# Two subtractions moved to GpSimd, a ring of eight PSUM banks and a new order of the steady period in an attention and gate kernel

## The reference

```python
xn = _layernorm(x, axis=-1)
q, k, v = proj(Wq), proj(Wk), proj(Wv)            # of xn
scores = einsum('bhsd,bhtd->bhst', q, k)          # causal
attn = softmax(where(mask, -inf, scores) / sqrt(D))
s = einsum('bse,fe->bsf', attn @ v, Wo)
h = silu(einsum(xn, wg)) * einsum(xn, wu)         # hidden 768, int weights / 127
g = _silu(einsum('bsh,dh->bsd', h, wd))
out = x + s * g
```

## Time and profile before

| | us |
|---|---|
| median of 3 runs (945.82 to 946.13) | 945.88 |
| the profiled execution's own time | 947.55 |
| its span, first to last instruction | 945.8 |
| TensorE busy | 914.8 (97%) |
| VectorE busy | 707.2 (75%) |
| ScalarE busy | 585.8 (62%) |
| GpSimd busy | 495.1 (52%) |

### The profile page before, as it was taken

How to read it: one execution, slowest core, us unless ns; L and a number is a source line. 1 busy time by engine, 2 the same in 40 slices (tenths; PEclk the granted TensorE clock), 3 DMA queues, 4 the chain that set the end, 5 groups by cost and what they waited for, 6 DMA issues and landing times.

```text
span 945.8 us, 22760 instructions
## 1 busy us (share of the span) xinstructions
PE 914.8 (97%) x9065; PEld 685.6 (72%) x9065; DVE 707.2 (75%) x950; ACT 585.8 (62%) x796; POOL 495.1 (52%) x681
## 2 busy tenths in 40 slices
PE   3999999999999999999999999999999999999995
PEld 2777767776868777686877868777786867768654
DVE  5985868778696887868788786877778697776823
ACT  5356664757576675756657575665757557575771
POOL 4253553736456464645636455473745547364553
PEclk9999999999999999999999999999999999999999
DMA  6704235353353534535343453534345253543323
GB/s 221 213 25 170 84 116 169 100 198 132 134 164 127 170 106 179 154 125 171 129 151 126 170 152 117 176 132 158 130 148 162 104 185 120 175 131 135 118 93 98
DMA packets 84507, 133.97 MB, mean 142 GB/s; under 512 B 13680, under 2 KB 34928, under 8 KB 84336
## 3 DMA queue, kind: packets, MB, share of 16 engines
q1 hardware_dynamic: 84400, 132.47, 41.8%
HBM read 53.22 MB, written 25.75 MB: 83 GB/s over the span
## 4 chain that ended last, share of the span: by engine, by line
PE 91%; DVE 2%; DMA 2%; POOL 2%; issue 1%; ACT 1%; SPq 0%; POOLq 0%; ACTq 0%; DVEq 0%
PE bank L194 48%; PE values L525 15%; PE bank L434 12%; PE bank L492 11%; PE bank L447 4%; DMA o_reciprocals<-scratch_r 1%; ACT probs L500 1%; DVE row_max L457 1%; PE bank L463 1%; POOL o_compact L566 1%; PE bank L668 0%; DMA scratch_r<-sum_reciprocals 0%; DVE x_in L259 0%; DVE xt_lo L279 0%; DMA sums<-scratch_o 0%
## 5 line engine op out<-in xcount | busy, mean ns | idle before, releaser
L457 DVE TENSOR_REDUCE row_max<-bank 128x2 f32<-128x768 f32 (+3 forms) x352 | 384.9, 1124 | 63.5 <-PE bank L447 60.3
L500 ACT ACTIVATE probs<-bank 128x1024 f32<-128x1024 f32 x320 | 320.4, 1026 | 122.2 <-PE bank L492 120.8
L507 POOL TENSOR_SCALAR_AFFINE_SELECT probs<-probs 128x256 f32<-128x256 f32 (+1 forms) x448 | 194.0, 450 | 275.1 <-ACT probs L500 274.1
L525 PE MATMUL values<-probs,v 128*17 128x512 f32 (+3 forms) x2048 | 166.2, 436 | 0.9 <-POOL probs L507 0.9
L393 POOL TENSOR_TENSOR h_lo<-gated,h_hi 128x512 fp32r<-128x512 f32 x96 | 124.6, 1298 | 74.8 <-ACT h_hi L390 72.7
L434 PE MATMUL bank<-k_stack,q_stack 64*128 64x128 f32 (+3 forms) x1024 | 155.3, 363 | 1.5 <-DVE row_max L457 1.2
L492 PE MATMUL bank<-q_stack,k_stack 64*128 64x512 f32 (+3 forms) x1024 | 142.2, 350 | 1.3 <-DVE row_max L457 0.7
L434 PEld LDWEIGHTS bank<-k_stack,q_stack 64*128 64x128 f32 x1024 | 83.1, 186 | 66.9 <-issue 30.4
L492 PEld LDWEIGHTS bank<-q_stack,k_stack 64*128 64x128 f32 x1024 | 82.9, 186 | 39.1 <-issue 17.3
L366 DVE SCALAR_TENSOR_TENSOR gated<-gated,bank 128x512 f32<-128x512 f32 x96 | 65.8, 685 | 55.4 <-ACT gated L363 55.4
L194 PE MATMUL bank<-xt_hi,wg_hi 128*128 128x256 f32 x384 | 99.3, 293 | 1.6 <-DVE gated L379 1.6
(11 more groups left out here) (123 smaller groups left out, 1624.4 us busy)
## 6 DMA issues: line engine op xcount, KB each, us to landing
k_stack<-qk_hi SPq DMA_DIRECT2D x64, 256.0 KB, 2.5
q_stack<-qk_hi SPq DMA_DIRECT2D x64, 256.0 KB, 2.5
scratch_o<-o SPq DMA_DIRECT2D x64, 256.0 KB, 2.2
x_again<-x SPq DMA_DIRECT2D x16, 512.0 KB, 4.7
k_stack<-qk_lo SPq DMA_DIRECT2D x32, 256.0 KB, 2.5
q_stack<-qk_lo SPq DMA_DIRECT2D x32, 256.0 KB, 2.6
o_compact<-scratch_o SPq DMA_DIRECT2D x32, 256.0 KB
o_reciprocals<-scratch_r SPq DMA_DIRECT2D x32, 256.0 KB
```

The source lines that it names most:

```text
L457: signal(e.tensor_reduce(rows, scores, axis=AX.X, op=ALU.max), "d_sm")
L500: signal(e.activation(PR[:, (SCORES * beta + k) % SLOTS, :, :], both(banks), ACT.Exp, scale=SCALE_S), "d_ex")
L507: last = e.affine_select(out=diag, in_=diag, compare_op=ALU.is_ge, fill=0.0, base=0, pattern=[[0, many], [1, P]], channel_multiplier=-1)
L525: last = nc.tensor.matmul(PVB[32 * c:32 * c + VW, j * P:S], V[par][:, j, 4 * g + c, :], PR[:, (SCORES * beta + 5 * g + kind) % SLOTS, pari ...
```

## The change

1. The low part of x (`lx`) and of the attention output (`os`) are subtracted by GpSimd instead of VectorE, in all three tables.
2. The bank of its own for values is gone. PSUM is one ring of 8 banks, and each `pv` entry names its bank. In HEAD and TAIL that is always bank 7, so only the name changes there; `pv` waits by `prev` now.
3. PERIOD has a new order and new banks. TAIL differs in two places: `os 1 1` now stands behind `on 1 1`, and the last `op` names bank 7 as well.

```diff
-RELEASED = dict(..., st="d_ex")
-RING = 7
+RELEASED = dict(..., st="d_ex", pv="d_ov")
+RING = 8
...
 PERIOD = table("""
-    ld 2 0, on 0 0, zr 0 0, ob 0 0, pv 0 11, sm 1 16 45, lt 2 0, st 1 1 01, la 2 0, st 1 2 23, mk 1 16 45, lm 2 0, gg 1 3 6,
+    on 0 0, ld 2 0, ob 0 0, lt 2 0, pv 0 11 7, lm 2 0, la 2 0, st 1 1 01, st 1 2 23, sm 1 16 45, mk 1 16 45, gu 1 2 6,
...
 TAIL = table("""
...
-    hs 1 4, ob 1 1, gu 1 5 0, hs 1 5, zr 0 0, os 1 1, xr 1 0, zr 1 0, on 1 1, dn 1 1 6, op 1 0 1, op 1 1 4""")
+    hs 1 4, ob 1 1, gu 1 5 0, hs 1 5, zr 0 0, xr 1 0, zr 1 0, on 1 1, os 1 1, dn 1 1 6, op 1 0 1, op 1 1 47""")
...
-        PVB = ctx.enter_context(nc.psum_tensor("values", [P, 512], FP32))
...
 def u_lx: 
-            elif en == "dve":
+            elif en == "pool":
                 after(e, "d_xh", beta, 1)
                 e.tensor_tensor(r(XT[1][:]), XTR[:], XT[0][:], ALU.subtract).then_inc(sems["d_xl"], 2)
...
 def u_pv:
                 if part == 0:
-                    after(e, "d_ov", beta, g - 1)
+                    prev(e)
...
-                            last = nc.tensor.matmul(PVB[32 * c:32 * c + VW, j * P:S], V[par][:, j, 4 * g + c, :],
+                            last = nc.tensor.matmul(PS[32 * c:32 * c + VW, banks[0], j * P:S], V[par][:, j, 4 * g + c, :],
...
-                signal(e.activation(O[:], PVB[:], ACT.Copy), "d_ov")
+                signal(e.activation(O[:], PS[:, banks[0], :], ACT.Copy), "d_ov")
...
 def u_os:
-            elif en == "dve":
+            elif en == "pool":
                 after(e, "d_oh", beta, k)
                 signal(e.tensor_tensor(r(OT[1][:, k, :]), OC[:], OT[0][:, k, :], ALU.subtract), "d_ol")
...
-                return PVB[:, 0:E] if halves and j == 1 else PS[:, banks[0], j * E:(j + 1) * E]
+                return PS[:, banks[1], 0:E] if halves and j == 1 else PS[:, banks[0], j * E:(j + 1) * E]
...
-                    users.update((n, (kind, b + ahead, k)) for n in banks)
+                    users.update((n, (kind, b + ahead, k // 3 if kind == "pv" else k)) for n in banks)
```

More of the change, by code:

```diff
@@ new lines @@
+    st 1 7 23, sm 1 21 45, mk 1 21 45, st 1 8 01, v 2 0 6, mt 1 1 2, gg 2 0 3, pv 1 3 7, sm 2 0 01, sm 2 1 45, or 0 1,
+    mk 2 0 01, hs 1 5, ob 0 1, mk 2 1 45, st 1 9 23, qk 2 2 6, pv 1 4 7, st 1 10 23, st 1 11 45, on 0 1, sm 2 2 01, mk 2 2 01,
+    pv 1 5 7, gu 2 0 6, st 1 12 01, st 1 13 34, os 0 1, od 1 0, pv 1 6 7, sm 2 3 01, mk 2 3 01, sm 2 4 56, mk 2 4 56, st 1 14 34,
+    qk 2 3 2, ls 2 2, dn 1 1 3, sm 2 5 56, st 1 15 01, pv 1 7 7, or 1 0, mk 2 5 56, sm 2 6 34, ls 2 3, st 1 16 01, mk 2 6 34,
@@ L80 @@
+    op 0 0 2, sm 2 7 01, st 1 17 45, mk 2 7 01, op 0 1 6, sm 2 8 45, hs 2 0, sm 2 9 01, mk 2 8 45, st 1 18 23, pv 1 8 7,
     mk 2 9 01, sm 2 10 45, sm 2 11 23, xr 1 0, mk 2 10 45, mk 2 11 23, st 1 19 01, gg 2 1 6, mt 2 0 4, sm 2 12 01,
[L81 to L82 removed]
+    mk 2 12 01, gu 2 1 5, v 2 1 3, sm 2 13 01, mk 2 13 01, sm 2 14 45, hs 2 1, mk 2 14 45, gg 2 2 6, pv 1 9 7, sm 2 15 01,
@@ L84 @@
+    mk 2 15 01, st 2 0 34, pv 1 10 7""")
 PERIOD = table("""
[L85 to L88 removed]
@@ new lines @@
+    gg 1 3 7, st 1 3 01, lc 2 0, sm 1 17 23, gu 1 3 4, mk 1 17 23, sm 1 18 56, st 1 4 01, mk 1 18 56, hs 1 2, gg 1 4 7,
+    gu 1 4 4, gg 1 5 2, zr 0 0, gu 1 5 3, lb 2 0, sm 1 19 01, st 1 5 56, od 0 1, mk 1 19 01, pv 1 0 7, pv 1 1 7, sm 1 20 23,
+    st 1 6 01, sm 1 21 45, lx 2 0, mk 1 20 23, os 0 0, mk 1 21 45, dn 1 0 6, mt 1 1 0, pv 1 2 7, pv 1 3 1, hs 1 3, st 1 7 23,
+    st 1 8 45, ls 2 0, st 1 9 67, qk 2 0 0, ls 2 1, v 2 0 2, hs 1 4, qk 2 1 3, hs 1 5, or 0 1, gg 2 0 4, gg 2 1 5, gg 2 2 6,
@@ new lines @@
+    ob 0 1, qk 2 2 7, st 1 10 23, st 1 11 45, pv 1 4 1, pv 1 5 1, st 1 12 67, sm 2 0 23, od 1 0, mk 2 0 23, sm 2 1 45,
+    ls 2 2, on 0 1, mk 2 1 45, qk 2 3 0, gu 2 0 1, sm 2 2 67, os 0 1, sm 2 3 23, sm 2 4 45, mk 2 2 67, mk 2 3 23, mk 2 4 45,
+    dn 1 1 0, st 1 13 67, sm 2 5 12, sm 2 6 34, ls 2 3, mk 2 5 12, mk 2 6 34, op 0 0 5, op 0 1 6, sm 2 7 01, st 1 14 23,
+    mk 2 7 01, sm 2 8 45, mk 2 8 45, pv 1 6 7, st 1 15 23, xr 1 0, sm 2 9 01, mk 2 9 01, hs 2 0, pv 1 7 7, pv 1 8 7,
+    sm 2 10 45, mk 2 10 45, or 1 0, st 1 16 23, st 1 17 01, gu 2 1 6, mt 2 0 7, st 1 18 45, sm 2 11 23, mk 2 11 23,
@@ new lines @@
+    sm 2 12 01, hs 2 1, mk 2 12 01, v 2 1 6, sm 2 13 45, st 1 19 23, mk 2 13 45, pv 1 9 7, sm 2 14 01, mk 2 14 01, st 2 0 23,
+    sm 2 15 45, mk 2 15 45, pv 1 10 7""")
+TAIL = table("""
+    ob 0 0, st 1 1 23, sm 1 16 45, on 0 0, mk 1 16 45, st 1 2 01, pv 0 11 7, sm 1 17 56, od 0 1, mk 1 17 56, st 1 3 34,
+    sm 1 18 12, mk 1 18 12, os 0 0, pv 1 0 7, st 1 4 56, st 1 5 01, sm 1 19 34, mk 1 19 34, gu 1 2 2, st 1 6 56, sm 1 20 01,
+    mk 1 20 01, hs 1 2, pv 1 1 7, pv 1 2 7, sm 1 21 45, mk 1 21 45, st 1 7 01, st 1 8 23, or 0 1, pv 1 3 7, mt 1 1 4, st 1 9 56,
+    dn 1 0 0, on 0 1, pv 1 4 7, ob 0 1, pv 1 5 7, st 1 10 34, st 1 11 56, gg 1 3 1, os 0 1, st 1 12 34, st 1 13 56, pv 1 6 7,
+    od 1 0, or 1 0, st 1 14 01, st 1 15 34, gu 1 3 2, st 1 16 56, st 1 17 01, pv 1 7 7, st 1 18 34, pv 1 8 7, ob 1 0, op 0 0 6,
+    st 1 19 34, on 1 0, pv 1 9 7, pv 1 10 7, pv 1 11 7, od 1 1, op 0 1 0, os 1 0, hs 1 3, gg 1 4 2, gu 1 4 3, or 1 1, gg 1 5 3,
+    hs 1 4, ob 1 1, gu 1 5 0, hs 1 5, zr 0 0, xr 1 0, zr 1 0, on 1 1, os 1 1, dn 1 1 6, op 1 0 1, op 1 1 47""")
@@ L806, in _ @@
             e.wait_ge(s_zeros, 1)
-            nc.tensor.matmul(PVB[:], ZERO[:, 0:P], ZERO[:], start=True, stop=True).then_inc(s_fixed, 1)
+            nc.tensor.matmul(PS[:, RING - 1, :], ZERO[:, 0:P], ZERO[:], start=True, stop=True).then_inc(s_fixed, 1)
             run("pe", e)
```

39 lines of the change are left out of this document (10 added, 29 removed).

## The result

The changed kernel takes **984.4 us** (median of 4 runs, 981.5 to 986.1) against 945.9 beside it: ratio 1.0395, 95% interval 1.0374 to 1.0415. That is 37 us above the forecast and outside the range. The profiled execution took 981.5 us, its span is 979.7. In three pieces, from the first matmul of a piece to the first of the next, the tail to the end of the span: head 153.17 us (before 151.51; it starts 1.2 us sooner in the span), 13 periods of 58.04 on average (before 55.79; they vary now from 55.9 to 60.2), tail 59.34 (before 55.05). So 29 of the 34 us by which the span grew are in the periods.

A forecast was written before the change was run, and what follows sets the result against it. TensorE was taken to bound the kernel, busy 914.8 of 945.8 us. Periods -2.6, head +1.6 and tail +2.5 sum to +1.5 on the median of 945.88: forecast 947.4 us, range 943 to 952.

The forecast's parts named there:

- the bullet on `o_lo`: Periods: output's low part takes 1.30 us on GpSimd for 0.7 on VectorE; SyncE's queue stands until 19.3; no cost.
- TensorE's clock: Periods: TensorE busy for all 55.80 us of a period at full granted clock; no term for a lower clock.
- the forecast's own -2.6: Periods: 13 x -0.2 us from the new matmul order, bounds -5 and +1.
- The order: Periods: new matmul order changes neighbouring array shapes, -0.2 us a period, between run count (0) and lowest sum (-0.3).
- The ring: Periods: values in bank 7 and, three times, bank 1 find them free with 0.3 us or more; no cost.
- The rival's bank: Periods: bank 4 comes late behind a row maximum on VectorE, 0.3 us each, 951.3 us; chance 0.36.
- `xt_lo`: Periods: x's low part on GpSimd takes about 2.43 us, done at 18.0, reader at 19.0; one us slack, no cost.
- Head: Head: x's low part ends later on GpSimd at two places, 0.3 and 1.35 us; +1.6 us, bounds 0.5 and 2.5.
- Tail: Tail: both last low parts of the output end later on GpSimd, +1.9 and +0.6 us; +2.5 us, bounds 2 to 3.
- Contention: Head and tail: moving the subtractions ends GpSimd's contention with VectorE over SBUF; undisturbed times used, such as 1.30 us for 1.82.
- The marks: Trace signs: periods 55.4 to 55.7 us without TensorE idle; wrong if under 55.3, over 55.9, or idle each period.

The follow-up runs named there:

- e10: Changed kernel with the output's first-half split early (before scores 4) and the load of x again moved into the next step: 948.3 us, ratio 0.999 to 1.002.
- e4: Changed kernel with the load of x again placed behind the next step's row maxima on SyncE's queue: 972.5 us, ratio 1.025 to 1.031.
- e9: Changed kernel with the load of x again moved into the next step, behind the sums' copy: 982.6 us, ratio 1.031 to 1.042.
- e13: e10 with the subtractions of the head and of the last two steps' output on VectorE: 943.4 us, ratio 0.995 to 0.998.
- e3: Kernel before the change with its values bank named as bank 7 of a ring of 8, order and subtractions as before: 946.9 us, ratio 0.999 to 1.001.
- e11: e10 with GpSimd computing the power for the statistics of x ahead of the product with the reciprocals: 951.2 us, ratio 1.003 to 1.007.

## Why the prediction was wrong

- **The step that failed** is the bullet on `o_lo`: "SyncE's queue stands until then with the rows of maxima behind it; they are wanted at 27.6 ... No cost." The stand was seen, its end nearly right (19.3; measured 20.05), and what it delays directly is little: in e10, which has not got it, the first stack copies leave 0.3 us sooner and the second half's product `on 0 1` starts at 34.6 for 35.3 (medians). The second `o_lo` ends at 38.6 and not at 37, just in time. But SyncE's queue was priced for this one thing behind this one stand. The working has no term for the load of x again, which stands in the same queue ahead of the next row maxima and waits for both stores. The new order makes the output's product late (38.7 in the prediction itself, 33.8 before), six copies leave right ahead of the stores, and the stores land 3.9 and 5.1 us after issue (2.2 and 2.6 before). So the load leaves at 50.4 for 44.3, and the maxima, ready at 49.9, leave at 52.2 (medians): TensorE waits 20.9 us for them in 13 periods.
- **What tests it**: with the load out of the way of the maxima, e4 has no such wait; with the first stand gone too and the load in the free stretch (e10), the periods are at 55.69, and the kernel is 0.8 us over the one beside it, where +1.5 was forecast. e10 is another kernel, so this shows the missing term and not that the forecast was right. What the load costs where it leaves together with other copies (e4, e9) is told only by their times to landing; no run moves one of them alone.
- **A second term that was missing** is TensorE's clock, taken as full in all periods. Four of the changed kernel's periods hold a stretch at 1.2 GHz (last section) and have 56.8 to 57.9 us of busy time where the others have 55.5 to 56.0, some 6 us in all. With 25 us of idle time and the forecast's own -2.6 this comes to 28 of the 29 us.
- **The order**, -0.2 us a period: held. The shortest step of each unit over 13 periods, added up, is 55.18 us after and 55.38 before. Where the waits are gone it shows: 55.39 in e13 and 55.69 in e10, of which 0.3 is idle time, against 55.79.
- **The ring**: free, by e3, which tries it in the old order. The rival's bank, behind `mk 1 16`, was no wait; four waits for another bank (`qk_lo`) add up to 2.6 us.
- **`xt_lo`**: 2.42 us (forecast 2.43), from 16.4 to 18.8 of the period (18.0 forecast), reader at 19.05. The slack was 0.25 and not 1, and it cost nothing.
- **Head**: +1.66, forecast +1.6.
- **Tail**: +4.3, forecast +2.5. The first low part starts where the addition ends, as forecast, 2.0 us later counted from the tail's start; the second starts 3.0 later, of which 0.5 is a longer last copy of the reciprocals (4.61 us, 4.13 before), and is 0.6 longer. The rest, 0.7, was not in the sum: the last product's matmuls take 415 ns each and not 279, at a granted clock of 0.72 for 0.95 in its window, which is partly the lower of the two levels, 1.2 GHz (0.50 from 971.0 to 974.2). TensorE had been idle 3.9 and 2.6 us shortly before (3.3 and 1.3 in the kernel before).
- **Contention**: the addition in the tail takes 1.29 us where it took 1.82 beside VectorE's subtraction. The Trainium skill (GPSIMD Engine Reference, Key points), which the prediction named for this, agrees with the row.
- **The marks**: "a period of 55.4 to 55.7 with TensorE without idle time" failed, and of the signs of being wrong a period over 55.9 and idle time in each period came; what ended it was the copy of the row maxima, not VectorE's maximum. `xt_lo` took 2.4 us, but its reader started 0.25 behind it and not 1; the head's `xt_lo` ended at 120.45, which counted from the first matmul is 121.7 on the old clock (121.5 named); the tail's first `o_lo` started where named, but from there to the end it is 24.9 us for 22.6, and not 0.6 more. No rival named SyncE's queue, and the range was built from edges of 0.1 to 0.3 us on banks, so it could not reach 984.

What stays open: why the periods of the changed kernel vary between 55.9 and 60.2 us. TensorE's idle time makes up 0.2 to 3.3 us of a period and the lower clock up to 2.4, and the queue's copies land at uneven times, but what sets the unevenness was not tried. Nor was it tried why the six stack copies behind `od 1 0` land late: the first six of the kernel before leave as close together and land after 2.4 to 2.8 us. Nor was e11's loss against e10 (3 us of median, at nearly equal periods) traced.

## What to carry to other kernels

Walk the queue that issues DMAs as carefully as an engine: list each wait in it, what stands behind that wait, and what those things wait for themselves. Here a load that waits for stores held row maxima that were ready, and a later product had made the stores late. When a table is written for an operation on one engine, order and engine are one change: each tried alone cost 20 and 81 us here, and undoing half of the move cost as much as undoing all of it (41 to 44 us). Two edits may show little one at a time (2 and 12 us) and 36 together: here the one freed the stretch of the queue in which the other could do no harm.
